# A two-layer decoder in one kernel: the quantised ffn's x is rounded on GpSimd, Silu is one instruction, the down product leaves by ScalarE

## The reference

```python
def _quant_dequant(v, axis):
    scale = jnp.max(jnp.abs(v), axis=axis, keepdims=True) / QMAX     # QMAX 127
    scale = jnp.maximum(scale, EPS)
    q = jnp.clip(jnp.round(v / scale), -QMAX, QMAX)
    return q * scale
...
xq = _ste(x, axis=-1)            # the quantised value, forward
w1q = _ste(w_gate_up, axis=-1)
gate_up = jnp.einsum('bsh,oh->bso', xq, w1q)
gate, up = (gate_up[..., :I], gate_up[..., I:])      # I = 704
h = jax.nn.silu(gate) * up
hq = _ste(h, axis=-1)
w2q = _ste(w_down, axis=-1)
return jnp.einsum('bsi,oi->bso', hq, w2q)            # 256 features, added to x
```

## Time and profile before

| | |
|---|---|
| median of 3 runs | 3353.1 us (3346.36 to 3360.9) |
| the profiled execution | 3374.1 us, span 3372.3 us |
| granted TensorE clock, mean | 0.921 of full speed |
| first gate evacuation of the last block | at 3126.6 us of the span |
| VectorE, ScalarE, GpSimd, TensorE busy in the span | 62%, 46%, 47%, 80% |

### The profile page before, as it was taken

How to read it: one execution, slowest core, us unless ns; L and a number is a source line. 1 busy time by engine, 2 the same in 40 slices (tenths; PEclk the granted TensorE clock), 3 DMA queues, 4 the chain that set the end, 5 groups by cost and what they waited for, 6 DMA issues and landing times. The chain is left out here.

```text
span 3372.3 us, 87461 instructions
## 1 busy us (share of the span) xinstructions
PE 2711.7 (80%) x33324; PEld 1938.6 (57%) x33324; DVE 2098.2 (62%) x3786; ACT 1544.7 (46%) x2686; POOL 1580.4 (47%) x1643
## 2 busy tenths in 40 slices
PE   1788888888858888877677768999999999996665
PEld 1666666666642222214466657887888788885332
DVE  4777777777748788848577743444444344444786
ACT  2555555555526677741233433333333333332665
POOL 1777777777742223214222224545455454542333
PEclk9899999999987799869799979999999999998666
DMA  3000000000012233200000000000000000000000
GB/s 114 1 1 0 0 0 0 0 0 0 0 31 76 81 92 93 88 26 0 24 27 25 25 19 5 7 7 5 7 5 7 5 7 5 7 2 27 13 19 19
DMA packets 94067, 73.28 MB, mean 22 GB/s; under 512 B 17314, under 2 KB 88354, under 8 KB 93218
## 3 DMA queue, kind: packets, MB, share of 16 engines
q1 hardware_dynamic: 93860, 70.14, 6.9%
HBM read 51.76 MB, written 17.04 MB: 20 GB/s over the span
## 5 line engine op out<-in xcount | busy, mean ns | idle before, releaser
L1303 DVE TENSOR_REDUCE x_mx<-x_ps 128x2 f16<-128x512 f32 x512 | 333.8, 683 | 70.9 <-PE x_ps L1367 68.4
L1272 ACT ACTIVATE x_e<-x_ps 128x512 f32<-128x512 f32 x512 | 292.6, 596 | 66.3 <-PE x_ps L1371 47.6
L1646 ACT ACTIVATE x_sq<-x_ps 128x512 f32<-128x512 f32 x256 | 152.3, 596 | 315.9 <-PE x_ps L1785 309.1
L1367 PE MATMUL x_ps<-x_k,x_q 32*128 32x256 f16 x1024 | 204.4, 304 | 76.7 <-ACT x_e L1272 43.8
L1367 PEld LDWEIGHTS x_ps<-x_k,x_q 32*128 32x128 f16 x1024 | 57.5, 94 | 276.9 <-DVE x_mx L1303 137.0
L103 PE MATMUL x_ps<-x_chi,x_w 128*128 128x128 f16 x1024 | 204.3, 224 | 14.4 <-ACT x_rkb L1667 7.5
L554 POOL TENSOR_TENSOR a_w<-a_qsw,a_tab 128x512 f32<-128x512 f32 x128 | 192.0, 1500 | 39.2 <-ACT a_qsw L614 39.2
L103 PE MATMUL a_ps<-a_wo,a0oh 128*128 128x256 f16 x512 | 140.9, 275 | 82.9 <-DVE a0ol L441 82.9
L1371 PE MATMUL x_ps<-x_q,x_k 32*128 32x256 f16 x1024 | 205.9, 305 | 1.7 <-ACT x_e L1272 1.4
L104 PE MATMUL x_ps<-x_clo,x_w 128*128 128x128 f16 x1024 | 203.6, 223 | 0.0
L105 PE MATMUL x_ps<-x_chi,x_w 128*128 128x128 f16 x1024 | 203.5, 223 | 0.0
(11 more groups left out here) (343 smaller groups left out, 9387.3 us busy)
## 6 DMA issues: line engine op xcount, KB each, us to landing
x_q<-x_q_rows SPq DMA_DIRECT2D x32, 256.0 KB, 2.8
x_k<-x_k_rows SPq DMA_DIRECT2D x32, 256.0 KB, 3.1
a_stage<-in_x_w SPq DMA_DIRECT2D x32, 256.0 KB, 2.6
x_vt<-in_ctx_v SPq DMA_DIRECT2D x32, 144.0 KB, 2.3
x_all<-in_x SPq DMA_DIRECT2D x8, 512.0 KB, 7.8
x_cf<-in_ctx SPq DMA_DIRECT2D x32, 128.0 KB, 2.1
x_q_rows<-x_xhl SPq DMA_DIRECT2D x32, 128.0 KB, 1.7
x_k_rows<-x_chl SPq DMA_DIRECT2D x32, 128.0 KB, 1.8
```

Source lines behind the costliest of these rows:

```text
L1272: act.activation(e[:, u % ES].rearrange("p c n -> p (c n)"), s2_ps(u), ACT.Exp, scale=XT ** -0.5).then_inc(e_ready, 1)
L1303: dve.reduce_max(mx[:, p % 2, c:c + 2], s1_ps(u), AX).then_inc(mx_ready, 1)
L1367: return pe.matmul(s1_ps(u)[:, c], q[r, p % 4, g, c * P:(c + 1) * P], k[r, p % 4, g], start=True, stop=True)
L1646: act.activation(sq[:, e % 4, :], ps[:, bank(e), :], ACT.Square).then_inc(act_left, 1)
```

## The change

Four things, all in `ffn_quantised`:

1. ScalarE applies Silu to gate, in place of Sigmoid, and VectorE multiplies it by `up`. GpSimd's product `gate_up` is gone.
2. GpSimd rounds x, in three `tensor_tensor` instructions of 256 (x times the reciprocal scale, plus and minus the rounding constant, with the [128, 1] operand broadcast), in place of ScalarE's two.
3. ScalarE evacuates the down product times its token's scale (`y_scaled`, into `yt`, now two buffers). GpSimd multiplies it by `s2` and adds the result into x (`add`, two instructions of 256), in place of VectorE's two.
4. The orders change. VectorE: h of t and its scale ahead of the scale of x of t+2. GpSimd: after the statistics chain of t+2 the rounding of t+2, then the add of t-1. ScalarE: Silu of t, transposed x of t+1, transposed h of t-1, normalise t+2, rounded h of t, y of t-1. In the head, GpSimd rounds tiles 0 and 1 only after both statistics chains. After the last tile the add runs on GpSimd.

```diff
--- before.py
+++ after.py
@@ -2253,7 +2253,6 @@
         gate = sb("gate", [P, FF])
         up = sb("up", [P, FF])
         sig = sb("sig", [P, FF])
-        gate_up = sb("gate_up", [P, FF])
         h = sb("h", [P, FF])
         hr = sb("hr", [P, FF])
         rnd = sb("rnd", [P, 2, 1])
@@ -2261,8 +2260,10 @@
         minus, minus_mean = sb("minus", [P, 1]), sb("minus_mean", [P, 1])
         hq = sb("hq", [P, 2, C2 * P], BF16)
         ht = sb("ht", [P, C2, P], BF16)
-        yt = sb("yt", [P, DM])
-        chain, zeroed, gup = sem("chain"), sem("zeroed"), sem("gup_ready")
+        yt = sb("yt", [P, 2, DM])
+        ys = sb("ys", [P, DM])
+        xm = sb("xm", [P, DM])
+        chain, zeroed = sem("chain"), sem("zeroed")
         xq_ready, xtp_ready, xt_ready, gu_ready, gate_ready, up_ready, sig_ready, hq_ready = (
             sem(n) for n in ("xq_ready", "xtp_ready", "xt_ready", "gu_ready", "gate_ready", "up_ready", "sig_ready", "hq_ready"))
         htp_ready, ht_ready, y_ready, yt_ready, x_done = (sem(n) for n in ("htp_ready", "ht_ready", "y_ready", "yt_ready", "x_done"))
@@ -2274,6 +2275,7 @@
         halves = lambda a: a.rearrange("p (k n) -> p k n", k=2)
         started = lambda t: not (isinstance(t, int) and t < 1)
         further = lambda t: not (isinstance(t, int) and t + 2 >= TILES)
+        hmul_ready, xm_ready, ys_ready = sem("hmul_ready"), sem("xm_ready"), sem("ys_ready")
         rnd_set, xs_ready, xr_ready, hs_ready, hr_ready = (sem(n) for n in ("rnd_set", "xs_ready", "xr_ready", "hs_ready", "hr_ready"))
         minus_set, minus_ready, shift_ready = sem("minus_set"), sem("minus_ready"), sem("shift_ready")
         x_out = [sem(f"x_out{i}") for i in range(2)]
@@ -2307,6 +2309,28 @@
                 wait_used(pool, ln.xn_ready, t, 2)
                 pool.tensor_tensor(shift[:, p], minus_mean[:, :], ln.rstd[:, p], ALU.mult).then_inc(shift_ready, 1)
 
+            def x_quantised(t, p):
+
+                wide = lambda a: a.to_broadcast([P, DM])
+                pool.wait_ge(xs_ready, t + 1)
+                wait_used(pool, xr_ready, t, 1)
+                pool.tensor_tensor(xm[:, :], ln.xn[:, p], wide(stat[:, p, 2:3]), ALU.mult).then_inc(xm_ready, 1)
+                pool.wait_ge(xm_ready, t + 1)
+                wait_used(pool, xq_ready, t, 1)
+                pool.tensor_tensor(xr[:, :], xm[:, :], wide(rnd[:, 0]), ALU.add).then_inc(xr_ready, 1)
+                pool.wait_ge(xr_ready, t + 1)
+                wait_used(pool, xtp_ready, t, 2)
+                pool.tensor_tensor(xq[:, p], xr[:, :], wide(rnd[:, 1]), ALU.add).then_inc(xq_ready, 1)
+
+            def add(t, p):
+                pool.wait_ge(yt_ready, t + 1)
+                wait_used(pool, x_done, t, 1)
+                pool.tensor_tensor(ys[:, :], yt[:, p], s2[:, :], ALU.mult).then_inc(ys_ready, 1)
+                pool.wait_ge(ys_ready, t + 1)
+                x = m.x_all[:, at(t), :]
+                ys_ = ys[:, :] if isinstance(t, int) else ys[:, :].rearrange("p (a n) -> p a n", a=1)
+                pool.tensor_tensor(x, x, ys_, ALU.add).then_inc(x_done, 1)
+
             def head():
                 pool.memset(minus[:, :], -1.0).then_inc(minus_set, 1)
                 ln.pool(pool)
@@ -2314,14 +2338,19 @@
                 mean_shift(0, 0)
                 ln.pool_step(pool, 1, 1)
                 mean_shift(1, 1)
+                pool.wait_ge(rnd_set, 2)
+                x_quantised(0, 0)
+                x_quantised(1, 1)
 
             def step(t, p, has_next):
                 if further(t):
                     ln.pool_step(pool, t + 2, p)
                     mean_shift(t + 2, p)
-                pool.wait_ge(up_ready, t + 1)
-                pool.tensor_tensor(gate_up[:, :], gate[:, :], up[:, :], ALU.mult).then_inc(gup, 1)
+                    x_quantised(t + 2, p)
+                if started(t):
+                    add(t - 1, 1 - p)
             over_tiles(pool, head, step)
+            add(TILES - 1, 1)
 
         @block.scalar
         def _(act):
@@ -2338,17 +2367,14 @@
             def normalise(t, p):
 
                 act.wait_ge(shift_ready, t + 1)
-                wait_used(act, xs_ready, t, 2)
+                wait_used(act, xm_ready, t, 2)
                 act.activation(ln.xn[:, p], m.x_all[:, at(t), :], ACT.Identity, scale=ln.rstd[:, p],
                                bias=shift[:, p]).then_inc(ln.xn_ready, 1)
 
-            def x_quantised(t, p):
-
-                act.wait_ge(xs_ready, t + 1)
-                act.activation(xr[:, :], ln.xn[:, p], ACT.Identity, scale=stat[:, p, 2:3], bias=rnd[:, 0]).then_inc(xr_ready, 1)
-                act.wait_ge(xr_ready, t + 1)
-                wait_used(act, xtp_ready, t, 2)
-                act.activation(xq[:, p], xr[:, :], ACT.Identity, bias=rnd[:, 1]).then_inc(xq_ready, 1)
+            def y_scaled(t, p):
+                act.wait_ge(y_ready, t + 1)
+                wait_used(act, ys_ready, t, 2)
+                act.activation(yt[:, p], y_ps(p), ACT.Copy, scale=hstat[:, p, 1:2]).then_inc(yt_ready, 1)
 
             def h_quantised(t, p):
                 act.wait_ge(hs_ready, t + 1)
@@ -2359,28 +2385,30 @@
 
             def head():
                 act.wait_ge(rnd_set, 2)
-                for t in range(2):
-                    normalise(t, t)
-                    x_quantised(t, t)
-                    x_transposed(t, t)
+                normalise(0, 0)
+                normalise(1, 1)
+                x_transposed(0, 0)
 
             def step(t, p, has_next):
-                if further(t):
-                    normalise(t + 2, p)
                 act.wait_ge(gate_ready, t + 1)
-                act.activation(sig[:, :], gate[:, :], ACT.Sigmoid).then_inc(sig_ready, 1)
+                wait_used(act, hmul_ready, t, 1)
+                act.activation(sig[:, :], gate[:, :], ACT.Silu).then_inc(sig_ready, 1)
+                if has_next:
+                    x_transposed(t + 1, 1 - p)
                 if started(t):
                     h_transposed(t - 1)
                 if further(t):
-                    x_quantised(t + 2, p)
-                    x_transposed(t + 2, p)
+                    normalise(t + 2, p)
                 h_quantised(t, p)
+                if started(t):
+                    y_scaled(t - 1, 1 - p)
             over_tiles(act, head, step)
             h_transposed(TILES - 1)
+            y_scaled(TILES - 1, 1)
 
         @block.vector
         def _(dve):
-            ch = Chain(dve, chain, 6, 6, 3)
+            ch = Chain(dve, chain, 6, 5, 3)
 
             def scale(v, st):
                 ch.link(dve.tensor_reduce(st[:, 0:1], v, AX, ALU.max, apply_absolute_value=True))
@@ -2394,18 +2422,11 @@
             def make_h(t, p):
 
                 dve.wait_ge(sig_ready, t + 1)
-                dve.wait_ge(gup, t + 1)
+                dve.wait_ge(up_ready, t + 1)
                 wait_used(dve, hr_ready, t, 1)
-                ch.link(dve.tensor_tensor(h[:, :], gate_up[:, :], sig[:, :], ALU.mult))
+                dve.tensor_tensor(h[:, :], up[:, :], sig[:, :], ALU.mult).then_inc(hmul_ready, 1)
+                dve.wait_ge(hmul_ready, t + 1)
                 scale(h[:, :], hstat[:, p]).then_inc(hs_ready, 1)
-
-            def add(t, p):
-                dve.wait_ge(y_ready, t + 1)
-                wait_used(dve, x_done, t, 1)
-                dve.scalar_tensor_tensor(yt[:, :], y_ps(p), hstat[:, p, 1:2], s2[:, :], ALU.mult, ALU.mult).then_inc(yt_ready, 1)
-                dve.wait_ge(yt_ready, t + 1)
-                x = m.x_all[:, at(t), :]
-                dve.tensor_tensor(x, x, yt[:, :], ALU.add).then_inc(x_done, 1)
 
             def head():
                 dve.memset(rnd[:, 0], ROUND).then_inc(rnd_set, 1)
@@ -2426,13 +2447,10 @@
                                          ALU.mult, ALU.mult).then_inc(gate_ready, 1)
                 dve.scalar_tensor_tensor(halves(up[:, :]), up_ps, stat[:, p, 1:2], halves(s1[:, FF:]),
                                          ALU.mult, ALU.mult).then_inc(up_ready, 1)
+                make_h(t, p)
                 if further(t):
                     scale_x(t + 2, p)
-                make_h(t, p)
-                if started(t):
-                    add(t - 1, 1 - p)
             over_tiles(dve, head, step)
-            add(TILES - 1, 1)
 
         @block.tensor
         def _(pe):
@@ -2461,7 +2479,7 @@
 
             def down(t, p):
                 pe.wait_ge(ht_ready, t + 1)
-                wait_used(pe, x_done, t, 2)
+                wait_used(pe, yt_ready, t, 2)
                 for c in range(C2):
                     k = P if c < C2 - 1 else tail
                     last = pe.matmul(y_ps(p), ht[0:k, c, :], w2[0:k, c, :], start=c == 0, stop=c == C2 - 1)
```

## The result

The changed kernel takes 3332.2 us (median of 5 runs, 3329.7 to 3349.1), the kernel before 3353.5 (median of 5): a ratio of 0.9945, 95% interval 0.9924 to 0.9966. It is faster by some 0.55%, at the edge of what can be told apart. The forecast was 3344.6, range 3325 to 3366.

What follows compares the result with a forecast made beforehand. VectorE's order was taken to bound the quantised ffn at 7.46 us a tile, then GpSimd's loop at 7.12. 27 tiles save 9.2, the ends +1.7 and -1.0: 8.5 less than 3353.1, so 3344.6 us, range 3325 to 3366.

Steps and rivals of the forecast that it cites:

- the rival without a collision: Quantised ffn: h comes after GpSimd's add has begun, or GpSimd is faster; 6.61 us a tile, 3331 us; chance 0.15.
- The bound and the new loop: Quantised ffn: VectorE's program order set 7.46 us a tile; GpSimd's work plus the round trip takes over at 7.12.
- roundings: GpSimd's three roundings of x: 0.61 to 0.62 us each, ending 2.14 us after the scale is ready.
- The collision: VectorE's h and GpSimd's full-width instructions exclude each other; GpSimd's add ends at 4.22, not 3.70; loop 6.61 plus 0.51.
- The ends of the stage: First and last tiles of the quantised ffn: +1.7 us at the head and -1.0 at the tail.
- Head: Stage start: GpSimd rounds tile 0 later, first gate moves by 2.8 us; +1.7 at tile 2, bounds 0 to +4.
- Tail: Stage end: no gate_up wait in the last two tiles, but a longer last add; -1.0 us, bounds -2 to +1.
- The sum: Whole stage: 27 x (7.46 - 7.12) = 9.2 us less, +1.7 - 1.0 at the ends: 8.5 us less.
- VectorE's wait for x: Sign in the changed stage's timeline: VectorE waits about 1 us a tile for ScalarE's normalised x.
- the rival with table switches: ScalarE: Silu's table lacks Identity or Copy, two loads a tile, 2.6 us more; 3355 to 3366 us; chance 0.05.
- the slower rival: VectorE's evacuations of gate and up hold the port, delaying GpSimd's roundings; 8.5 us a tile, 3382 us; chance 0.08.
- `h` ahead of GpSimd's product: h gets the port first and holds GpSimd's yt x s2 product; 7.58 to 7.8 us a tile, 3357 to 3363; chance 0.14.

Runs made afterwards that it cites:

- the second: The changed kernel as it is, run again, 12 runs: 3338.5 us against 3350.4 for the kernel before, ratio 0.9959.
- e2: Changed kernel, but h multiplies Silu by the up product straight from PSUM, without its scale: 6.47 us a tile, ratio 0.9933 to the kernel before.
- e1: Kernel before with Silu alone: VectorE multiplies it by up, GpSimd's gate_up product gone, nothing moved: 6.83 us a tile, ratio 0.9942 to the kernel before.
- e10: e3 with one more VectorE reduction (0.87 us) in each tile, read by nobody: 6.36 us a tile, one run.
- e5: Changed kernel with one more GpSimd product of 256 elements in each tile, read by nobody: 7.57 us a tile, one run.
- e3: Changed kernel with GpSimd's two adds of tile t-2 behind the statistics chain instead of ahead: 5.58 us a tile, 3299.0 us, ratio 0.9835 to the kernel before.

## Why the prediction was right

**What the time alone says: little.** The range, 3325 to 3366, takes in two of the rivals, and 3332.2 is within 2 us of the 3331 that the rival without a collision gave; the forecast was 3344.6. The first median is also 21 us below the kernel before, past the 17 us for which the prediction gave a chance of 0.23; the second, 12 below, is not. That the forecast's mechanism held and not that rival's is read from the stage: a period of 7.00, where the rival has 6.61, and the long rows of `h` and the add.

**The bound and the new loop: right, and near in size.** 7.12 forecast, 7.00 measured. Term by term, in the ring shown above: roundings end 2.07 after the scale (2.14 forecast); the add ends at 4.09 (4.22); the normalisation starts at 5.41 (5.67); the next scale is ready at 6.86 (7.12). The roundings cost 612 ns as the line through 128 and 512 elements said. What was off is small: gaps between GpSimd's instructions of 0.08, not 0.1, and between its statistics and the normalisation 1.36 in that tile, not 1.45. The other tile of each turn takes 7.14, and the mean is the 7.00.

**The collision: right in size, in half the tiles by another form.** 0.51 forecast (its own terms, 4.22 less 3.70, give 0.52), 0.53 by e2. In half the tiles its form was right: `h` at 1.11, where I had written 1.2 to 1.4; in the others `h` arrives in the gap, some 0.4 us later than I had placed it, since VectorE issues its turn of the loop there (0.36 us of issue ahead of its statistics). The add takes 1.23 on average (1.2 forecast). That the two forms, 0.42 and 0.62, average to what was forecast is luck: the prediction priced the first alone.

**The ends of the stage: mis-sized.** Head, first statistics to the gate of tile 2: 21.74 before, 21.67 after, so -0.1 and not +1.7. The first gate did move, by 2.6 us (2.8 forecast). The two tiles behind it took 10.8 us, not 13.5; the table for Silu was loaded while TensorE made the first gate product, and cost nothing:

```profile
3116.47 1.28 ACT L2395 ACT_TABLE_LOAD   x1
...
3116.51 2.53 PE L2469 MATMUL f_ps<-f_w,f_xt 128*128 128x352 bf16 x8 [0.46 <-ACT f_xt L2360]
```

Tail, from the gate of tile 29 to the end: 25.4 and 23.0, -2.4 and not -1.0. Together -2.5 where I had +0.7.

**The sum.** 27 tiles at the forecast 0.34 gave 9.2; measured 12.5 (201.4 and 188.9 us from gate 2 to gate 29). With the ends, 15.0 against 8.5. The direction and the mechanism held and the size was low by 6.5 us, half of it in the period and half at the ends. The medians moved by 21 us in the first set and 12 in the second, on either side of 15.0.

**The other rivals.** VectorE's wait for x was 1.27 (1 forecast). Silu took 0.79, and the table load above is the only one in the block, so the rival with table switches is out: Silu, Identity and Copy ran on that one load. The rows of gate and `up` stayed at 0.94 beside GpSimd's roundings, and the roundings at 0.61:

```profile
3206.75 0.92 DVE L2446 SCALAR_TENSOR_TENSOR f_gate<-f_ps,f_stat,f_s 128x704 f32<-128x704 f32 x1
...
3206.99 0.61 POOL L2320 TENSOR_TENSOR f_xr<-f_xm,f_rnd 128x256 f32<-128x256 f32 x1
```

So these evacuations out of PSUM and GpSimd's reads don't exclude each other, and the slower rival is out. `h` ahead of GpSimd's product didn't occur in the steady tiles.

**What the prediction didn't see.** That Silu alone gives as much (e1). It was in its own numbers: 7.46 less the wait of 0.52 is 6.94, already less than its own 7.12. And that the loop it named could be opened by moving one call: it said that GpSimd's work and the round trip add up, but not that nothing forces them to.

## What to carry to other kernels

Where each engine runs in order, the period is the longest ring, and that can go through several engines, none of them the busiest, or lie in one engine's own order (as in e10). Look for waits that go round (here GpSimd for VectorE, VectorE for ScalarE, ScalarE for GpSimd), and put independent work of the same engine into the round trip rather than ahead of it. Here that was worth 1.42 us of 7.00 a tile, three times what the change brought, 0.5 of it because the collision went too. Before moving work off the bounding engine, price the wait that is inside its order: removing one dependence (GpSimd's product) gave more than the whole change did. A VectorE multiply of two SBUF tiles that met GpSimd's two adds cost GpSimd's loop 0.5 us a tile.

## What the runs showed of the hardware

GpSimd's cost of a `tensor_tensor` of 256 elements depends on how many tiles it reads: 728 ns for two, 608 for the same tile twice (e5) and 612 with a broadcast second operand (both in the groups above).

A VectorE multiply of two SBUF tiles and GpSimd's work on SBUF tiles exclude each other, in order of arrival (the two forms under e2); with one operand of the multiply in PSUM both are at their free cost (892 and 726 ns in e2, 998 and 1229 in the changed kernel).

TensorE's granted clock differed between kernels although TensorE wasn't the bound. From 3150 to 3250 us the matmuls of gate and up took, in the changed kernel and in e3:

```profile
L2469 PE MATMUL f_ps<-f_w,f_xt 128*128 128x352 bf16 x112 | 34.5, 488 | 0.1
```

```profile
L2471 PE MATMUL f_ps<-f_w,f_xt 128*128 128x352 bf16 x146 | 34.5, 395 | 0.8
```

The first is the changed kernel, the second e3. In this stretch e3 has a mean granted clock of 0.84 and the changed kernel 0.62; 1.0 stands for 2.4 GHz and 0.5 for 1.2. TensorE's busy share is about the same in both (63% and 64%), but at the higher clock more instructions stand in it (398 and 308). What decides the level wasn't tried. In both, TensorE waits for the rounded x, 2.5 us a tile in the changed kernel and 1.9 in e3.
